# Two buffers instead of one for the activation quantizer of a two-layer transformer kernel

## The chip, the cores and the metric

The kernel runs on the eight cores of one Trainium2 chip, each core on one of the eight sequences of the batch. The metric is the device time of one launch in microseconds (us), taken at the slowest core. The engines of a core are named TensorE (PE in the profile), VectorE (DVE), ScalarE (ACT), GpSimd (POOL) and SyncE (SP), which issues the transfers.

## The reference

A core computes two pre-norm transformer layers on its [2048, 1024] sequence: attention, a feed-forward with one matrix, a latent attention, and a feed-forward with a hidden width of 4096. The part that this case is about is the feed-forward of layer 0, whose input is quantized to whole numbers between -128 and 127 and whose weight is quantized to -1, 0 and 1:

```python
w_scale = jnp.mean(jnp.abs(weight)) + EPS
u = weight / w_scale
w_quant = jnp.clip(jnp.round(u), -1.0, 1.0)
a_scale = jnp.max(jnp.abs(x), axis=-1, keepdims=True) + EPS
z = jnp.clip(x / a_scale * 127.0, -128.0, 127.0)
a_quant = jnp.round(z)
y = jnp.einsum('bsi,oi->bso', a_quant, w_quant)
y = y * (w_scale * a_scale / 127.0)
...
x = x + _L0_attn_ref(_layernorm(x, axis=-1), ...)
x = x + _L0_ffn_ref(_layernorm(x, axis=-1), L0_ffn_weight)
```

## The kernel before

The residual stream stays in SBUF, transposed: eight tiles X0 to X7 of 128 features by 2048 tokens in float32. The kernel emits its stages one after the other, with a barrier of all engines between them: entry (transposes), layer norm and attention of layer 0 (`emit_l0a`), layer norm and feed-forward of layer 0 (`emit_l0f`), and the same two for layer 1. Beside X there is an arena of 104 KB per partition, in which each stage lays its own tiles at offsets written out by hand (`ov`).

Every instruction goes through `do` (line 55), a small recorder. It takes the keys that an instruction reads (`r`) and writes (`w`). For each key it knows the last writers and readers, and puts waits on their semaphores ahead of the instruction. The first writer of a key that the stage has not seen waits for all semaphores of the last barrier (`floor`). Each engine runs its instructions in the order of emission. Keys are names and not addresses, so two tiles can be used independently only if they have two keys. The semaphore counts of an engine are in the order of its instructions.

`emit_l0f` (line 684) first prepares weights, then finds for each token the largest absolute value of the normalized input, and leaves 127 divided by it in a row ROWR. Then comes the loop over four quarters qq of 512 tokens. A quarter begins with a broadcast of its piece of ROWR (TensorE, line 868), which VectorE copies to RAB (line 872). Then come eight steps, c = 0 to 7, one for each tile of 128 features:

- GpSimd makes the scaled input in the tile XN_: subtract the mean (line 313, in the helper `xn_into`), multiply by the inverse deviation (line 317), multiply by RAB (line 878).
- ScalarE adds 128.5 and writes U_ (line 883), and copies U_ to R_ (line 887).
- VectorE takes the whole part off R_ in eight pairs of instructions, for the powers 128, 64, ... 1: line 891 writes to B_ the power where R_ is at least that, line 894 subtracts B_ from R_. What is left in R_ is the fraction, and line 897 writes U_ - 128 - R_, the rounded value, to the slice c of AQW in bfloat16.

After the eight steps TensorE multiplies by the quantized weight WQ: eight output tiles of eight matmuls each (line 907). The first output tile takes each slice of AQW as soon as it is there. VectorE scales each result (line 922, with ASB from line 920) and GpSimd adds it to X (line 925). The next quarter's XN_ stands behind these additions on GpSimd's queue.

XN_, U_, R_ and B_ have one buffer each.

Of the kernel before, what the change touches and what calls it, by code (L numbers as in the profile page):

```python
# [7 lines left out]
F32 = mybir.dt.float32  # L8
BF16 = mybir.dt.bfloat16
AF = mybir.ActivationFunctionType  # L10
OP = mybir.AluOpType
# [4 lines left out]
NCH = 8  # L16
NQ = 4
QW = 512
# [14 lines left out]
class KB:  # L33
# [650 lines left out]
    def emit_l0f(self):  # L684
        s = self
# [6 lines left out]
        SB32 = s.ov("SB32", [32, 128], F32, 57 * 1024)  # L692
        RAB = s.ov("RAB", [128, QW], F32, 58 * 1024)
        ASB = s.ov("ASB", [128, QW], F32, 60 * 1024)
        U_ = s.ov("U_", [128, QW], F32, 62 * 1024)
        ROWR = s.ov("ROWR", [1, 4096], F32, 64 * 1024)
        WPA = s.ov("WPA", [128, T], F32, 82 * 1024)
        R_ = s.ov("R_", [128, QW], F32, 94 * 1024)
# [167 lines left out]
        for qq in range(NQ):  # L866
            s.do("tensor", lambda e, qq=qq, ROWR=ROWR:
                 e.matmul(s.PS[6][:], s.ONE1[0:1, :],
                          ROWR[0:1, QW * qq:QW * (qq + 1)], start=True, stop=True),
                 r=("ROWR", "one1"), w=("PS6",))  # L870
            s.do("vector", lambda e, RAB=RAB:
                 e.tensor_copy(RAB[:], s.PS[6][:]), r=("PS6",), w=("RAB",))
            for c in range(NCH):
                wx = ("XN00", "XN01", "XN02", "XN03") if qq == 0 and c == 0 \
                    else ()
                s.xn_into(XN_[:], "XN", c, qq, eng="gpsimd", wx=wx)
                s.do("gpsimd", lambda e, XN_=XN_, RAB=RAB:
                     e.tensor_tensor(XN_[:], XN_[:], RAB[:], OP.mult),  # L878
                     r=("XN", "RAB"), w=("XN",))
                uwx = ("XN10", "XN11", "XN12", "XN13") if qq == 0 and c == 0 \  # L880
                    else ()
                s.do("scalar", lambda e, U_=U_, XN_=XN_:
                     e.activation(U_[:], XN_[:], AF.Identity,  # L883
                                  bias=s.SM[:, 30:31], scale=1.0),
                     r=("XN", "SM30"), w=("U",) + uwx)
                s.do("scalar", lambda e, R_=R_, U_=U_:
                     e.activation(R_[:], U_[:], AF.Copy), r=("U",), w=("R",))
                for k in range(7, -1, -1):
                    val = float(1 << k)
                    s.do("vector", lambda e, val=val, B_=B_, R_=R_:  # L890
                         e.tensor_scalar(B_[:], R_[:], val, val, OP.is_ge, OP.mult),  # L891
                         r=("R",), w=("B",))
                    s.do("vector", lambda e, R_=R_, B_=B_:
                         e.tensor_tensor(R_[:], R_[:], B_[:], OP.subtract),  # L894
                         r=("R", "B"), w=("R",))
                s.do("vector", lambda e, c=c, U_=U_, R_=R_, AQW=AQW:
                     e.scalar_tensor_tensor(  # L897
                         AQW[:, QW * c:QW * (c + 1)],
                         U_[:], -128.0, R_[:], OP.add, OP.subtract),
                     r=("U", "R"), w=(f"AQc{c}",))  # L900
            for mch in range(NCH):
                bk = f"PS{mch % 2}"
                bank = s.PS[mch % 2]
                for kc in range(NCH):
                    s.do("tensor", lambda e, mch=mch, kc=kc, bank=bank,
                         WQ=WQ, AQW=AQW:
                         e.matmul(bank[:],  # L907
                                  WQ[:, 1024 * kc + 128 * mch:1024 * kc + 128 * (mch + 1)],
                                  AQW[:, QW * kc:QW * (kc + 1)],
                                  start=(kc == 0), stop=(kc == NCH - 1)),  # L910
                         r=("WQ", f"AQc{kc}"), w=(bk,))
                s.close_group(bk)
                if mch == 0:
                    s.do("tensor", lambda e, qq=qq, ROWR=ROWR:
                         e.matmul(s.PS[6][:], s.ONE1[0:1, :],
                                  ROWR[0:1, 2048 + QW * qq:2048 + QW * (qq + 1)],
                                  start=True, stop=True),
                         r=("ROWR", "one1"), w=("PS6",))
                    s.do("vector", lambda e, ASB=ASB:
                         e.tensor_copy(ASB[:], s.PS[6][:]), r=("PS6",), w=("ASB",))  # L920
                s.do("vector", lambda e, bank=bank, ASB=ASB, mch=mch:
                     e.tensor_tensor(s.SC[2 + mch % 2][:], bank[:], ASB[:], OP.mult),
                     r=(bk, "ASB"), w=(f"SC{2 + mch % 2}",))
                s.do("gpsimd", lambda e, mch=mch, qq=qq:
                     e.tensor_tensor(s.X[mch][:, QW * qq:QW * (qq + 1)],
                                     s.X[mch][:, QW * qq:QW * (qq + 1)],
                                     s.SC[2 + mch % 2][:], OP.add),
                     r=(f"SC{2 + mch % 2}", f"X{mch}q{qq}"), w=(f"X{mch}q{qq}",))
# [552 lines left out]
```

How the kernel before makes its waits and increments, by code:

```python
        def f(e, build=build, real=tuple(real), sn_inc=sn_inc, n=n):  # L99
            for (sn, v0) in real:
                e.wait_ge(sems[sn], v0)
            build(e).then_inc(sems[sn_inc], n)
# [19 lines left out]
    def barrier(self):  # L122
        self.flush_ep()
        self.do("sync", lambda e: e.nop(),
                xw=[(sn, self.cnt[sn]) for sn in (*self.LDS, *self.STS)])
        vals = {}
        for e in ENGS:
            vals[e] = self.do(e, lambda en: en.nop(),
                              xw=[(ESEM[e], self.cnt[ESEM[e]])], force=True)
        for e in ENGS:
            for o in ENGS:
                if o == e:
                    continue
                sn = ESEM[o]
                if self.hw[e].get(sn, 0) < vals[o]:
                    self.hw[e][sn] = vals[o]
                    self.th[e].append(
                        lambda en, sn=sn, v0=vals[o]: en.wait_ge(self.sems[sn], v0))
            for sn in (*self.LDS, *self.STS):
                self.hw[e][sn] = max(self.hw[e].get(sn, 0), self.cnt[sn])
        self.floor = {ESEM[o]: vals[o] for o in ENGS}
        for sn in (*self.LDS, *self.STS):
            self.floor[sn] = self.cnt[sn]
```

## Time and profile before

| | us |
|---|---|
| median of 4 timed runs | 8131.44 |
| lowest and highest of them | 7953.81 to 8172.14 |
| the profiled execution | 7675.34 |
| its span on the slowest core (core 5) | 7673.6 |
| the quantizing loop on core 5 | 2508 to 3099 of the span |

The profile is of one execution. Its times are those of the slowest core, counted from the first instruction. "Idle before" is the time an engine stood still ahead of an instruction, and the name behind the arrow is what ended it. The engines' busy shares are averages over stages with different limits.

### The profile page before, as it was taken

Reading aid. Unit: us, or ns where it says so; the run is one execution under the profiler, and the core shown is the slowest. Engines: PE = TensorE matmul, PEld = TensorE weight load, DVE = VectorE, ACT = ScalarE, POOL = GpSimd, SP = SyncE. Lnnn points to the kernel's source line nnn. Section 1 sums busy time; section 2 is a strip of 40 time slices with the busy share of each in tenths; the row PEclk is TensorE's granted clock in tenths of the full one; section 3 lists DMA queues with packets and bytes.
Section 4 is the critical chain, followed back from the end, with each engine's and each line's share of the span. In section 5 each row is a group of like instructions: output and inputs, shape, how many; then the busy total and the mean of one; then the engine's idle time right before and its main releaser. Section 6 shows DMA issues by size and latency. Waiting matters only on the chain.

```text
span 7673.6 us, 101772 instructions; the slowest of 8 cores (7660.7 to 7673.6 us)
## 1 busy us (share of the span) xinstructions
PE 5883.9 (77%) x15346; PEld 2147.0 (28%) x15346; DVE 2296.5 (30%) x3740; ACT 2055.7 (27%) x3076; POOL 616.7 (8%) x580
## 2 busy tenths in 40 slices
PE   6888988889863111769879988898678879789786
PEld 2333333333321000223222322222223323223232
DVE  1333213332105666121111111111133332342323
ACT  1333333333310000103223322232242241332420
POOL 0000000000002222000000000000021120210200
PEclk8888998889975555889889989898889989899896
DMA  1000000000011000000000000000012212122121
GB/s 54 1 1 1 1 1 1 1 1 1 1 42 47 1 0 0 17 1 1 1 7 1 1 1 1 1 1 1 9 61 72 68 61 80 60 67 75 59 75 67
DMA packets 58435, 179.42 MB, mean 23 GB/s; under 512 B 9723, under 2 KB 16294, under 8 KB 57894
## 3 DMA queue, kind: packets, MB, share of 16 engines
q1 hardware_dynamic: 57894, 172.92, 7.2%
q8 instruction: 253, 4.15, 0.2%
q14 instruction: 288, 2.36, 0.1%
HBM read 164.44 MB, written 8.39 MB: 23 GB/s over the span
## 4 chain that ended last, share of the span: by engine, by line
PE 68%; DVE 15%; issue 8%; ACT 4%; DMA 2%; POOL 1%; DVEq 1%; ACTq 0%; SPq 0%; POOLq 0%; PEldq 0%
PE PS L334 16%; PE PS L352 15%; PE PS L1300 11%; PE PS L1236 7%; DVE R__98 L894 3%; PE PS L340 2%; DVE W1L L1202 2%; DVE B__99 L891 2%; PE PS L359 2%; PE PS L279 2%; ACT W1H L1200 1%; PE PS L274 1%; PE PS L1000 1%; PE PS L985 1%; PE PS L945 1%
## 5 line engine op out<-in xcount | busy, mean ns | idle before, releaser
L346 ACT ACTIVATE E<-PS,SM 128x512 f32<-128x512 f32 x1280 | 864.0, 686 | 1361.4 <-PE PS L340 684.0
L363 DVE COPY RBF<-PS 64x512 f32<-64x512 f32 x128 | 88.2, 689 | 2252.4 <-PE PS L359 2183.4
L334 PE MATMUL PS<-QP,KHD 64*128 64x512 f32 x1280 | 746.3, 675 | 10.8 <-issue 10.6
L352 PE MATMUL PS<-E,VFB 128*128 128x512 f32 x1280 | 659.6, 611 | 4.9 <-ACT E L346 4.9
L352 PE MATMUL PS<-E,VFA 128*128 128x512 f32 x1280 | 656.7, 611 | 1.3 <-ACT E L346 1.3
L1236 PE MATMUL PS<-XNH,W1H 128*128 128x512 bf16 x1024 | 437.1, 427 | 184.0 <-ACT W1H L1200 145.1
L1236 PE MATMUL PS<-XNH,W1L 128*128 128x512 bf16 x1024 | 436.5, 426 | 121.2 <-DVE W1L L1202 104.7
L907 PE MATMUL PS<-AQW,WQB 128*128 128x512 bf16 x256 | 79.5, 453 | 500.5 <-DVE AQW L897 500.5
L1268 POOL TENSOR_TENSOR SC<-SC 128x512 f32<-128x512 f32 x128 | 161.6, 1263 | 3485.8 <-PE PS L1236 3437.0
L1236 PE MATMUL PS<-XNL,W1H 128*128 128x512 bf16 x1024 | 431.8, 422 | 0.4 <-DVE XNL L1184 0.2
L1300 PE MATMUL PS<-ACH,W1H 128*128 128x512 bf16 x1024 | 388.9, 380 | 34.6 <-ACT ACH L1279 34.4
L1300 PE MATMUL PS<-ACL,W1H 128*128 128x512 bf16 x1024 | 388.7, 380 | 9.5 <-POOL ACL L1286 4.2
L1300 PE MATMUL PS<-ACH,W1L 128*128 128x512 bf16 x1024 | 388.5, 379 | 0.2
L334 PE MATMUL PS<-QA,KA 128*128 128x512 f32 x640 | 338.0, 623 | 0.0
L334 PEld LDWEIGHTS PS<-QP,KHD 64*128 64x128 f32 x1280 | 204.5, 196 | 471.8 <-issue 469.3
L1220 DVE TENSOR_TENSOR W1L<-W2F,W1H 128x1024 bf16<-128x1024 f32 x128 | 157.3, 1229 | 585.3 <-PE PS L1300 544.1
L334 PE MATMUL PS<-QB,KB 128*128 128x512 f32 x640 | 321.5, 596 | 0.0
L1217 ACT ACTIVATE W1H<-W2F 128x1024 bf16<-128x1024 f32 x128 | 135.1, 1056 | 671.6 <-PE PS L1300 671.6
L352 PEld LDWEIGHTS PS<-E,VFB 128*128 128x128 f32 x1280 | 231.2, 192 | 297.3 <-issue 290.7
L352 PEld LDWEIGHTS PS<-E,VFA 128*128 128x128 f32 x1280 | 232.4, 192 | 290.5 <-issue 284.3
L1202 DVE TENSOR_TENSOR W1L<-W1F,W1H 128x1024 bf16<-128x1024 f32 x127 | 177.2, 1395 | 317.8 <-ACT W1H L1200 255.3
L883 ACT ACTIVATE U__95<-XN__100,SM 128x512 f32<-128x512 f32 x32 | 23.1, 722 | 825.9 <-POOL XN__100 L878 429.9
(235 smaller groups left out, 6783.4 us busy)
## 6 DMA issues: line engine op xcount, KB each, us to landing
W1F<-w1p SPq DMA_DIRECT2D x128, 512.0 KB, 3.5
W2F<-w SPq DMA_DIRECT2D x128, 512.0 KB, 3.9
TM<-x_in SPq DMA_DIRECT2D x16, 512.0 KB, 12.5
WTR<-w0T SPq DMA_DIRECT2D x16, 512.0 KB, 4.1
y_out<-XO SPq DMA_DIRECT2D x16, 512.0 KB, 2.6
WPA<-wo1T SPq DMA_DIRECT2D x16, 256.0 KB, 2.6
WPA<-wuq SPq DMA_DIRECT2D x8, 128.0 KB, 2.0
WPB<-wuk SPq DMA_DIRECT2D x8, 128.0 KB, 2.0
```

What stands on the lines that cost most here:

```text
L279: e.matmul(s.PS[5][:], s.ALL1[:], sq[:], start=(c == 0), stop=(c == NCH - 1)),
L334: e.matmul(s.PS[sb][:], k_lhsT(kc), q_rhs(qq), start=True, stop=not diag),
L340: e.matmul(s.PS[sb][:], s.I128B[:], s.MSK[:, QW * j:QW * (j + 1)], start=False, stop=True),
L346: e.activation(s.E32[eb][:], s.PS[sb][:], AF.Exp, bias=negc),
L352: e.matmul(pvbank[:], v_lhsT(kc), s.E32[eb][:], start=(kc == 0), stop=(kc == kcmax - 1)),
L359: e.matmul(s.PS[6][hs_ctx, :], s.I128[hs_z, hs_z], s.RBF[hs_z, :], start=True, stop=True),
L894: e.tensor_tensor(R_[:], R_[:], B_[:], OP.subtract),
L1202: e.tensor_tensor(w1l[:], w1f[:], w1h[:], OP.subtract),
L1220: e.tensor_tensor(w2l[:, 0:1024], w2f[:], w2h[:, 0:1024], OP.subtract),
L1236: e.matmul(bank[:], lh[:, FCW * kc:FCW * (kc + 1)], rh[:, QW * kc:QW * (kc + 1)], start=(kc == 0 and pi == 0), stop=(kc == 7 and pi == 2)),
L1268: e.tensor_tensor(s.SC[0][:], s.SC[0][:], s.SC[3][:], OP.add),
L1300: e.matmul(s.PS[mch][:], lh[:, 128 * mch:128 * (mch + 1)], rh[:, QW * kc:QW * (kc + 1)], start=(kc == 0 and pi == 0), stop=(kc == 31 and p ...
```

## The change

XN_, U_, R_ and B_ get a second buffer each (XN2, U2, R2, B2), at offsets of the arena that are free in this stage or, for B2 and XN2, held the weight tile WPB that was read out long before. The steps take the buffers in turn, by (8 qq + c) modulo 2, and each buffer has its own key. The first writers of the tiles in WPB's place (step 1 of the first quarter) also wait for WPB's readers. All instructions, their shapes and the order on every engine stay as they are.

```diff
--- before.py
+++ after.py
@@ -692,7 +692,16 @@
         SB32 = s.ov("SB32", [32, 128], F32, 57 * 1024)
         RAB = s.ov("RAB", [128, QW], F32, 58 * 1024)
         ASB = s.ov("ASB", [128, QW], F32, 60 * 1024)
-        U_ = s.ov("U_", [128, QW], F32, 62 * 1024)
+        UP = [s.ov("U_", [128, QW], F32, 62 * 1024),
+              s.ov("U2", [128, QW], F32, 100 * 1024)]
+        RP = [s.ov("R_", [128, QW], F32, 94 * 1024),
+              s.ov("R2", [128, QW], F32, 102 * 1024)]
+        BP = [s.ov("B_", [128, QW], F32, 96 * 1024),
+              s.ov("B2", [128, QW], F32, 24 * 1024)]
+        XNP = [s.ov("XN_", [128, QW], F32, 98 * 1024),
+               s.ov("XN2", [128, QW], F32, 26 * 1024)]
+        U_ = UP[0]
+        XN_ = XNP[0]
         ROWR = s.ov("ROWR", [1, 4096], F32, 64 * 1024)
         WPA = s.ov("WPA", [128, T], F32, 82 * 1024)
         R_ = s.ov("R_", [128, QW], F32, 94 * 1024)
@@ -871,33 +880,40 @@
             s.do("vector", lambda e, RAB=RAB:
                  e.tensor_copy(RAB[:], s.PS[6][:]), r=("PS6",), w=("RAB",))
             for c in range(NCH):
+                p = (qq * NCH + c) % 2
+                Ut, Rt, Bt, XNt = UP[p], RP[p], BP[p], XNP[p]
+                uk, rk, bk_, xk = f"Up{p}", f"Rp{p}", f"Bp{p}", f"XNp{p}"
                 wx = ("XN00", "XN01", "XN02", "XN03") if qq == 0 and c == 0 \
                     else ()
-                s.xn_into(XN_[:], "XN", c, qq, eng="gpsimd", wx=wx)
-                s.do("gpsimd", lambda e, XN_=XN_, RAB=RAB:
-                     e.tensor_tensor(XN_[:], XN_[:], RAB[:], OP.mult),
-                     r=("XN", "RAB"), w=("XN",))
+                if qq == 0 and c == 1:
+                    wx = ("WPB",)
+                s.xn_into(XNt[:], xk, c, qq, eng="gpsimd", wx=wx)
+                s.do("gpsimd", lambda e, XNt=XNt, RAB=RAB:
+                     e.tensor_tensor(XNt[:], XNt[:], RAB[:], OP.mult),
+                     r=(xk, "RAB"), w=(xk,))
                 uwx = ("XN10", "XN11", "XN12", "XN13") if qq == 0 and c == 0 \
                     else ()
-                s.do("scalar", lambda e, U_=U_, XN_=XN_:
-                     e.activation(U_[:], XN_[:], AF.Identity,
+                s.do("scalar", lambda e, Ut=Ut, XNt=XNt:
+                     e.activation(Ut[:], XNt[:], AF.Identity,
                                   bias=s.SM[:, 30:31], scale=1.0),
-                     r=("XN", "SM30"), w=("U",) + uwx)
-                s.do("scalar", lambda e, R_=R_, U_=U_:
-                     e.activation(R_[:], U_[:], AF.Copy), r=("U",), w=("R",))
+                     r=(xk, "SM30"), w=(uk,) + uwx)
+                s.do("scalar", lambda e, Rt=Rt, Ut=Ut:
+                     e.activation(Rt[:], Ut[:], AF.Copy), r=(uk,), w=(rk,))
                 for k in range(7, -1, -1):
                     val = float(1 << k)
-                    s.do("vector", lambda e, val=val, B_=B_, R_=R_:
-                         e.tensor_scalar(B_[:], R_[:], val, val, OP.is_ge, OP.mult),
-                         r=("R",), w=("B",))
-                    s.do("vector", lambda e, R_=R_, B_=B_:
-                         e.tensor_tensor(R_[:], R_[:], B_[:], OP.subtract),
-                         r=("R", "B"), w=("R",))
-                s.do("vector", lambda e, c=c, U_=U_, R_=R_, AQW=AQW:
+                    kwx = ("WPB",) if qq == 0 and c == 1 and k == 7 else ()
+                    s.do("vector", lambda e, val=val, Bt=Bt, Rt=Rt:
+                         e.tensor_scalar(Bt[:], Rt[:], val, val, OP.is_ge,
+                                         OP.mult),
+                         r=(rk,), w=(bk_,) + kwx)
+                    s.do("vector", lambda e, Rt=Rt, Bt=Bt:
+                         e.tensor_tensor(Rt[:], Rt[:], Bt[:], OP.subtract),
+                         r=(rk, bk_), w=(rk,))
+                s.do("vector", lambda e, c=c, Ut=Ut, Rt=Rt, AQW=AQW:
                      e.scalar_tensor_tensor(
                          AQW[:, QW * c:QW * (c + 1)],
-                         U_[:], -128.0, R_[:], OP.add, OP.subtract),
-                     r=("U", "R"), w=(f"AQc{c}",))
+                         Ut[:], -128.0, Rt[:], OP.add, OP.subtract),
+                     r=(uk, rk), w=(f"AQc{c}",))
             for mch in range(NCH):
                 bk = f"PS{mch % 2}"
                 bank = s.PS[mch % 2]
```

The order on ScalarE at the start of the quantizing loop, before: U from XN and R from U, each time the same tiles (the numbers behind the names are those of the allocations).

```order
L883 ACTIVATE U__95<-XN__100,SM 128x512
L887 ACTIVATE R__98<-U__95 128x512
L883 ACTIVATE U__95<-XN__100,SM 128x512
L887 ACTIVATE R__98<-U__95 128x512
L883 ACTIVATE U__95<-XN__100,SM 128x512
```

And with the change, at the same place:

```order
L897 ACTIVATE U__95<-XN__101,SM 128x512
L901 ACTIVATE R__97<-U__95 128x512
L897 ACTIVATE U2_96<-XN2_102,SM 128x512
L901 ACTIVATE R2_98<-U2_96 128x512
L897 ACTIVATE U__95<-XN__101,SM 128x512
```

Nothing moved; every second pair has other tiles. Lines 883, 887, 891, 894 and 897 of before are lines 897, 901, 906, 910 and 913 with the change.

## Rows read from the trace of the kernel before

**Rows 1.** All cores: span and mean granted TensorE clock
```profile
core 2: 7660.7 us, clock 0.853
...
core 5: 7673.6 us, clock 0.850
```

**Rows 2.** Page, part 1: busy time, share of the span, instructions
```profile
PE 5883.9 (77%) x15346; PEld 2147.0 (28%) x15346; DVE 2296.5 (30%) x3740; ACT 2055.7 (27%) x3076; POOL 616.7 (8%) x580
```

**Rows 3.** Groups of instructions, 2500 to 3100 us (busy, mean | idle before <-releaser)
```profile
L907 PE MATMUL PS<-AQW,WQB 128*128 128x512 bf16 x256 | 79.5, 453 | 500.5 <-DVE AQW L897 500.5
...
L891 DVE TENSOR_SCALAR B__99<-R__98 128x512 f32<-128x512 f32 x256 | 142.2, 556 | 102.1 <-ACT R__98 L887 70.2 <-POOL XN__100 L317 6.0 <-ACTq L128 1.8
L897 DVE SCALAR_TENSOR_TENSOR AQW<-U__95,R__98 128x512 bf16<-128x512 f32 x32 | 22.1, 692 | 13.1 <-issue 8.5 <-DVE R__98 L894 4.5
...
L872 DVE COPY RAB<-PS 128x512 f32<-128x512 f32 x4 | 2.8, 691 | 8.3 <-issue 7.0 <-PE PS L868 1.2
```

**Rows 4.** Stretches, core 5: busy time of each engine, clock, DMA
```profile
core 5: us, PE busy (x) PEld busy (x) DVE busy (x) ACT busy (x) POOL busy (x), PEclk, DMA share, GB/s
...
2666.00:2787.00 121.00, 4.97 (x9) 1.20 (x10) 92.03 (x136) 9.69 (x15) 27.14 (x21) 0.50 0.00 0
```

**Rows 5.** Waits, 2500 to 3100 us (waiting <- releaser: total us, times, longest)
```profile
ACT U__95 L883 <- DVE AQW L897: 396.0, 28, 15.1
...
DVE B__99 L891 <- ACT R__98 L887: 70.2, 30, 6.8
```

**Rows 6.** Timeline of a steady step (start, duration, [idle before])
```profile
2679.28 0.69 DVE L897 SCALAR_TENSOR_TENSOR AQW<-U__95,R__98 128x512 bf16<-128x512 f32 x1 [0.17 <-DVE R__98 L894]
2680.11 0.72 ACT L883 ACTIVATE U__95<-XN__100,SM 128x512 f32<-128x512 f32 x1 [13.89 <-DVE AQW L897]
...
2680.98 0.63 ACT L887 ACTIVATE R__98<-U__95 128x512 f32<-128x512 f32 x1
2681.04 1.26 POOL L313 TENSOR_TENSOR XN__100<-X,MU 128x512 f32<-128x512 f32 x1 [10.99 <-ACT U__95 L883]
2681.78 0.80 DVE L891 TENSOR_SCALAR B__99<-R__98 128x512 f32<-128x512 f32 x1 [1.82 <-ACT R__98 L887]
2682.51 1.26 POOL L317 TENSOR_TENSOR XN__100<-XN__100,RBC 128x512 f32<-128x512 f32 x1 [0.20 <-POOL XN__100 L313]
2682.69 1.62 DVE L894 TENSOR_TENSOR R__98<-R__98,B__99 128x512 f32<-128x512 f32 x1
2684.03 1.40 POOL L878 TENSOR_TENSOR XN__100<-XN__100,RAB 128x512 f32<-128x512 f32 x1 [0.26 <-POOL XN__100 L317]
2684.42 1.30 DVE L891 TENSOR_SCALAR B__99<-R__98 128x512 f32<-128x512 f32 x1
2685.82 0.69 DVE L894 TENSOR_TENSOR R__98<-R__98,B__99 128x512 f32<-128x512 f32 x1
...
2694.66 0.69 DVE L897 SCALAR_TENSOR_TENSOR AQW<-U__95,R__98 128x512 bf16<-128x512 f32 x1 [0.17 <-DVE R__98 L894]
```

**Rows 7.** Timeline, VectorE, the step c=7 of the second quarter
```profile
2774.48 0.43 DVE L891 TENSOR_SCALAR B__99<-R__98 128x512 f32<-128x512 f32 x1 [1.82 <-ACT R__98 L887]
2775.01 0.69 DVE L894 TENSOR_TENSOR R__98<-R__98,B__99 128x512 f32<-128x512 f32 x1
...
2785.19 0.69 DVE L897 SCALAR_TENSOR_TENSOR AQW<-U__95,R__98 128x512 bf16<-128x512 f32 x1 [0.17 <-DVE R__98 L894]
```

**Rows 8.** Timeline, start of the second quarter
```profile
2658.76 1.26 POOL L925 TENSOR_TENSOR X<-X,SC 128x512 f32<-128x512 f32 x1 [0.62 <-PE PS L868]
...
2659.98 1.26 POOL L313 TENSOR_TENSOR XN__100<-X,MU 128x512 f32<-128x512 f32 x1
...
2666.40 0.80 DVE L891 TENSOR_SCALAR B__99<-R__98 128x512 f32<-128x512 f32 x1 [6.79 <-ACT R__98 L887]
```

**Rows 9.** Line 363, the copy in the attention
```profile
L363 DVE COPY RBF<-PS x128: 682/689/697, 296.4 to 5423.9; 64x512 f32<-64x512 f32 x128
```

**Rows 10.** Timeline, TensorE, the end of the second quarter
```profile
2788.65 15.23 PE L907 MATMUL PS<-AQW,WQB 128*128 128x512 bf16 x56
```

## The prediction

> **What bounds the kernel now.** I first read the table of cores [rows 1]: all eight spans lie between 7660.7 and 7673.6 us at the same granted clock, about 0.85, so any core stands for all, and I use core 5. The page's busy shares [rows 2] say TensorE 77%, VectorE 30%, ScalarE 27%, GpSimd 8%. Over the whole program TensorE sets the time. But the change touches only the activation quantizer of layer 0's feed-forward, so the limit has to be read there. The groups of that stage [rows 3] show the opposite picture: TensorE's 256 matmuls of line 907 are busy 79.5 us and wait 500.5 us for the quantized tile AQW that VectorE writes on line 897. The table of stretches [rows 4] agrees: from 2666 to 2787 us (the quantizing part of the second quarter) VectorE is busy 92.03 of 121 us, TensorE 4.97, and the granted TensorE clock is 0.50, its level of 1.2 GHz, after an almost idle stretch. So in this stage every microsecond by which VectorE is late is a microsecond of the kernel, as long as it comes to an end in the matmuls at the quarter's end.
>
> What does VectorE wait for? The list of waits [rows 5] gives it in one line: 70.2 us in 30 waits of line 891 for ScalarE's R of line 887. ScalarE in turn waits 396.0 us, 28 times, for VectorE's line 897, since U and R have one buffer each. That is a closed ring: line 897 reads U and R, only then may ScalarE write the next U (0.72 us) and the next R (0.63 us), and only then can line 891 start. The timeline of one steady step [rows 6] shows it: line 897 starts at 2679.28 and ends at 2679.97, U starts at 2680.11, R at 2680.98, and line 891 starts at 2681.78 after an idle time of 1.82 us. The next step's line 897 starts at 2694.66: one step takes 15.38 us.
>
> The same rows show a second cost. The first three VectorE instructions of the step take 0.80, 1.62 and 1.30 us; line 894 later in the step takes 0.69, and where nothing disturbs them the two lines take 0.43 and 0.69 [rows 7]. They are long exactly while GpSimd's three multiplies run (2681.04, 2682.51 and 2684.03), and each ends 0.28 to 0.54 us after the GpSimd instruction that it met. The third GpSimd instruction starts while line 894 still runs and takes 1.40 instead of 1.26. So the two engines take turns, instruction by instruction. The stretch is 0.37 + 0.93 + 0.87 = 2.17 us. The step c=7, in which GpSimd does nothing [rows 7], has no stretch: it runs from 2774.48 to the end of line 897 at 2785.88, that is 11.40 us for the 17 instructions. Check: 1.82 + 11.40 + 2.17 = 15.39.
>
> **The change part by part.** The 17 VectorE, two ScalarE and three GpSimd instructions of a step remain, in the same order and with the same shapes; only the buffers alternate. A quarter has eight steps.
>
> (a) The wait goes. With two U and R, ScalarE can make step c+1's pair while VectorE works on c. Seven times per quarter 1.82 us leave VectorE's path: 12.7 us, and 51.0 us in four quarters. The first step of a quarter keeps its wait [rows 8]: 6.79 us at 2666.40, because its XN stands on GpSimd behind eight residual additions, which wait for the quarter's own matmuls. Nothing there changes. Nor do I see a wait that comes instead: ScalarE's queue holds U, R of c+1 ahead of U of c+2, and only the latter waits for VectorE.
>
> (b) The cover goes for part of GpSimd's work. Before, the first of the three multiplies of a step lay mostly in VectorE's idle time and cost only 0.37 us. Afterwards VectorE is never idle there. GpSimd gets two steps ahead: XN of c+4 is allowed when ScalarE has read XN of c+2, which waits for line 897 of step c. So at the start of a quarter GpSimd makes XN1, XN2, XN3 in one go (nine instructions; the first finds VectorE still waiting for ScalarE), and XN4 to XN7 fall into steps 1 to 4. That leaves 8 + 12 = 20 instructions which meet a busy VectorE, where before 21 met it, seven of them at the small price. The price of one meeting is 0.93 or 0.87 from [rows 6]; I take 0.90. A quarter's stretch is then 20 x 0.90 = 18.0 us against 7 x 2.17 = 15.2 before: 2.8 us more, 11.2 in all. In a formula, a quarter gains 12.7 + 15.2 - 20x. The bounds of x: above, the whole GpSimd instruction, 1.26 [rows 6]; below, the old total, 15.2 / 20 = 0.76. These give gains of 2.7 and 12.7 us a quarter, 11 and 51 in all. I take 0.90 since it is measured on the same pair of instructions.
>
> The Trainium skill ("SBUF — State Buffer", section on the two separate sides) speaks against the change more strongly: it calls the port pair that VectorE and GpSimd share an exclusive lock held for the full instruction, with the loser fully blocked. Taken as worded that is the end at 1.26 and a gain of 11 us instead of some 40; the trace agrees that they exclude each other but shows a price of 0.87 to 0.93, since part of each instruction passes before it is held.
>
> (c) ScalarE now runs U and R (1.35 us a step) beside a working VectorE; before, it ran while VectorE waited. Nothing in this stage shows that meeting. Its bounds: 0, and full exclusion, 28 x 1.35 = 38 us. The nearest row with ScalarE working almost without pause is the copy of line 363 in the attention [rows 9], 682 to 697 ns, mean 689; the copy of the same free size on line 872, with ScalarE idle, takes 691 [rows 3]. That row copies from PSUM, so it is near and not the same. I take 0.
>
> (d) First use of a name. The recorder makes the first writer of a new key wait for all semaphores of the last barrier. In the first quarter line 897 shows 1.07 us of idle time for that in each of eight steps (8.5 us, 8 times) [rows 3]. Those stay. The second B buffer adds one such wait on VectorE at step 1: +1.1 us. The second XN, U and R add theirs on GpSimd and ScalarE, which have over 10 us of slack. Bounds 0 to 4 us for the four keys. The additional waits on WPB's readers are met long before.
>
> (e) TensorE: after step 7 the quarter's last 56 matmuls take 15.23 us [rows 10]; unchanged. The steps before them arrive 11.5 to 14 instead of 15 us apart, still far from keeping TensorE busy.
>
> Sum: -51.0 + 11.2 + 0 + 1.1 = -38.7, say 39 us. The profiled execution took 7675.34 us (span 7673.6 and 1.7 around it), so it would take 7636. The median of the timed runs is 8131.44, 5.9% above that execution, and their own range is 7953.81 to 8172.14. No row shows where those 456 us lie. VectorE's durations do not hang on TensorE's clock, so I subtract the same 39 us: 8092.4, or -0.5%.
>
> **The rivals.** A: GpSimd costs its whole instruction at each meeting (x = 1.26), or ScalarE's 1.35 us are paid in part. Gain 0 to 25 us, time 8106 to 8131. For it: back-to-back instructions leave no gap for either engine. Against it: the two fully overlapped meetings in [rows 6] cost 0.93 and 0.87, with gaps on VectorE of only 0.10.
>
> B, the other side: at step 0 to 4 each GpSimd instruction holds up two VectorE instructions instead of one, because its 1.26 us is longer than line 891 plus its gap (0.53) and VectorE never drains its queue. Place: the 20 meetings of a quarter. Price x = 2 x 0.87 = 1.74, so 27.9 - 34.8 = -6.9 a quarter, 28 us slower, with (d) 29: 8160. It decides from x = 27.9 / 20 = 1.40. Against it: the three stretched instructions of a step are followed by one of 0.69 at once.
>
> C: the wait is removed but comes back, because ScalarE is still held: then line 891 shows 1.8 us again and the time is 8131 to 8132. The ring would have to be closed by another single buffer. AQW has one slice per step, its readers of the quarter before have finished, and SC is not in the ring. I find none.
>
> D: the change is right but the timed runs lie elsewhere. The runs before spread over 218 us, five times the forecast; one of four lies 2.2% under the median. A median of such runs can move by over 2% without any cause in this stage.
>
> **How the numbers follow.** My forecast (25 to 51 us gained): 0.75. A and C together: 0.15. B: 0.04. D: 0.06. The predicted time is 8092.4. About 2% of the time, 163 us, is what a measurement of this kernel can tell from no change; even the complete wait is 51. So faster by over 2% can come only from D (0.04), slower only from D or from B with D (0.02), and 0.94 is left for the middle. The range takes the spread of the runs with it: low 7953.8 - 39 = 7915, high 8172.1 - 6 = 8166, the 6 being a gain at the small end of A.
>
> **What would show it.** Right: line 891 waits for ScalarE four times only, some 20 us in place of 70.2; line 897 starts about 14.2 us apart in steps 1 to 4 and 11.5 in steps 5 to 7; step 0 grows from 13.6 to about 18.6 us with eight stretched instructions; the quarter from the first line 891 to the end of the eighth line 897 shrinks from 119.5 to about 109.6 us. Busy time of lines 891 and 894 grows by about 11 us. Wrong: steps 5 to 7 longer than 11.6 (then ScalarE costs something), stretched instructions over 2.0 us or more than 20 a quarter (rival B), a wait of 1.8 us that remains (rival C), or another stage whose time moved.

## The result and the profile after

| | before, us | changed, us |
|---|---|---|
| first timing, median | 8028.46 (10 runs, the 4 of above among them) | 8094.37 (7 runs) |
| first timing, lowest and highest | 7671.95 to 8172.14 | 7886.93 to 8157.04 |
| first timing, ratio and interval | | 1.0295 [1.0251, 1.0339] |
| later timing (e9), ratio and interval | | 0.9918 [0.9873, 0.9964] |
| lowest time in the three later timings | 7671.33, 7673.51, 7672.18 | 7625.31, 7625.20, 7620.25 |
| profiled execution | 7675.34 | 7903.04 |

The two ratios contradict each other, and the first can't be understood without one fact about the executions: in many executions of either kernel TensorE's granted clock is lower on all four cores of one half of the chip (a die: cores 0 to 3 or 4 to 7), or of both, for a few hundred microseconds or more, and in the first timing every execution of the changed kernel had that, the seven of the table and seven more on record (7834.48 to 8182.49 us), while the profiled execution before had it on no core. The profiled execution of the changed kernel shows it. Its cores, span and mean granted clock:

```profile
core 0: 7893.4 us, clock 0.814
...
core 2: 7668.5 us, clock 0.809
...
core 5: 7743.6 us, clock 0.803
...
core 7: 7901.5 us, clock 0.813
```

All eight cores had 0.850 to 0.853 before [rows 1]. The next two rows are the stretch from the start to just ahead of the changed loop, for core 7 and for core 2 of the same execution (TensorE, its weight loads, VectorE, ScalarE and GpSimd busy, then the granted clock):

```profile
0.00:2500.00 2500.00, 2191.03 (x4346) 846.94 (x4346) 647.93 (x1094) 764.09 (x1177) 87.36 (x76) 0.76 0.02 7
```

```profile
0.00:2490.00 2490.00, 1982.12 (x4533) 787.10 (x4533) 758.45 (x1327) 756.29 (x1177) 141.20 (x195) 0.85 0.04 12
```

Up to here every engine runs the same instructions as before. Core 7 got 0.76 of the clock there and has done less at its end: VectorE has worked through 1094 instructions against 1327 on core 2. Its loop starts 272 us later (first line 906 at 2785.3 against 2513.4), and that is nearly all of the 281 us by which its span exceeds that of a core with the clock of before (7620.8, see e9). So the 7901.5 us of this profile do not come from the instructions of the changed loop. Two stretches of core 7 inside the attention, the first of the kernel before and the second of the changed kernel, show the level of the clock:

```profile
540.00:680.00 140.00, 135.68 (x324) 56.34 (x322) 16.47 (x27) 55.59 (x85) 0.00 (x0) 1.00 0.00 1
```

```profile
590.00:750.00 160.00, 157.44 (x308) 63.32 (x306) 16.41 (x27) 52.50 (x79) 0.00 (x0) 0.81 0.00 1
```

With TensorE busy nearly all the time in both, 1.00 of the clock is granted before and 0.81 here, and 2.3 matmuls a microsecond end before and 1.9 here. Core 2 had the clock of the kernel before up to the loop (0.85 against 0.86 on the same core) and a lower one only behind it (0.82 against 0.89); it is the core on which the loop can be compared.

The groups, on core 2 (lines 906, 910 and 913 are 891, 894 and 897 of before; a group with the second buffers is listed as B, R, U), and TensorE's group on the page (core 7, its loop is 4 us longer):

```profile
L906 DVE TENSOR_SCALAR B__99<-R__97 128x512 f32<-128x512 f32 x128 | 81.4, 636 | 37.4 <-ACT R__97 L901 19.5 <-POOL XN L892 6.0
L906 DVE TENSOR_SCALAR B<-R 128x512 f32<-128x512 f32 x128 | 69.1, 540 | 12.3 <-DVE AQW L913 0.4
...
L913 DVE SCALAR_TENSOR_TENSOR AQW<-U__95,R__97 128x512 bf16<-128x512 f32 x16 | 11.1, 693 | 6.3 <-issue 4.3 <-DVE R__97 L910 2.1
```

```profile
L923 PE MATMUL PS<-AQW,WQB 128*128 128x512 bf16 x256 | 81.7, 469 | 455.5 <-DVE AQW L913 444.6
```

In [rows 3] line 891 was busy 142.2 us and waited 70.2 for R. Now the two groups of line 906 are busy 81.4 + 69.1 = 150.5 us and wait 19.5: the busy time has grown by 8.3, the wait has shrunk by 50.7. The stretches of lines 906 and 910 (what their instructions take beyond 0.43 and 0.69 us) are together 70.4 us, against 58.5 of lines 891 and 894 on core 5 before. TensorE's wait for AQW on VectorE went from 500.5 to 444.6. The waits in the loop, on core 2, answer to [rows 5]:

```profile
ACT U__95 L897 <- DVE AQW L913: 161.0, 12, 14.9
...
ACT U L897 <- DVE AQW L913: 143.3, 12, 13.9
...
DVE B__99 L906 <- ACT R__97 L901: 19.5, 3, 6.5
```

VectorE waits for R three times, at the starts of quarters 2 to 4, for 6.5 us each where it was 6.8 [rows 8]; the other 27 are gone. ScalarE still waits 24 times for VectorE's line 913, as it should: it is now a step ahead. The stretch of the second quarter answers to [rows 4]:

```profile
2653.00:2763.00 110.00, 4.24 (x8) 0.83 (x8) 94.67 (x136) 10.09 (x16) 26.99 (x21) 0.50 0.00 0
```

VectorE is busy 94.67 of 110 us where it was busy 92.03 of 121. A whole step, to be read against [rows 6]:

```profile
2671.73 0.69 DVE L913 SCALAR_TENSOR_TENSOR AQW<-U__95,R__97 128x512 bf16<-128x512 f32 x1 [0.17 <-DVE R__97 L910]
2672.34 0.42 DVE L906 TENSOR_SCALAR B<-R 128x512 f32<-128x512 f32 x1
2672.57 0.72 ACT L897 ACTIVATE U__95<-XN__101,SM 128x512 f32<-128x512 f32 x1 [14.58 <-DVE AQW L913]
...
2672.86 0.69 DVE L910 TENSOR_TENSOR R<-R,B 128x512 f32<-128x512 f32 x1
...
2673.49 1.26 POOL L313 TENSOR_TENSOR XN__101<-X,MU 128x512 f32<-128x512 f32 x1 [7.80 <-ACT U__95 L897]
2673.66 1.38 DVE L906 TENSOR_SCALAR B<-R 128x512 f32<-128x512 f32 x1
2674.96 1.26 POOL L317 TENSOR_TENSOR XN__101<-XN__101,RBC 128x512 f32<-128x512 f32 x1 [0.20 <-POOL XN__101 L313]
2675.14 1.63 DVE L910 TENSOR_TENSOR R<-R,B 128x512 f32<-128x512 f32 x1
2676.49 1.40 POOL L892 TENSOR_TENSOR XN__101<-XN__101,RAB 128x512 f32<-128x512 f32 x1 [0.27 <-POOL XN__101 L317]
2676.88 1.30 DVE L906 TENSOR_SCALAR B<-R 128x512 f32<-128x512 f32 x1
...
2685.79 0.69 DVE L913 SCALAR_TENSOR_TENSOR AQW<-U,R 128x512 bf16<-128x512 f32 x1 [0.17 <-DVE R L910]
```

Line 906 starts at 2672.34, before line 913's recorded end of 2672.42, and U and R are made beside it. GpSimd's three instructions now all meet a working VectorE. The stretched ones are 1.38 (0.95 too long), 1.63 (0.94) and 1.30 (0.87). Each ends 0.28, 0.55 and 0.29 us after the GpSimd instruction that it met, that is its own 0.43 or 0.69 us less some 0.15. From line 913 to line 913 it is 14.06 us instead of 15.38.

The loop, from the first start of line 891 (now 906) to the last start of line 897 (now 913), took 563.1 to 565.3 us on the eight cores before, median 564.1. It takes 517.6 to 519.4 on cores 0 to 5 now, and 522.3 and 522.7 on cores 6 and 7. The gain is 45 to 46 us.

### The profile page after: what moved, and what is told of

The parts are those of the page before. It is cut to its first block, busy times and chain, and to the rows that moved or that the text cites. A ratio compares the mean times of both kernels' runs of the same rounds, so it can differ in the third digit from the quotient of the medians.

```text
span 7901.5 us, 101825 instructions; the slowest of 8 cores (7665.6 to 7901.5 us)
## 1 busy us (share of the span) xinstructions
PE 6180.3 (78%) x15346; PEld 2245.8 (28%) x15346; DVE 2300.6 (29%) x3740; ACT 2062.7 (26%) x3076; POOL 619.9 (8%) x580
## 4 chain that ended last, share of the span: by engine, by line
PE 70%; DVE 14%; issue 8%; ACT 3%; DMA 2%; DVEq 1%; POOL 1%; ACTq 0%; SPq 0%; POOLq 0%; PEldq 0%
PE PS L334 18%; PE PS L352 16%; PE PS L1316 11%; PE PS L1252 7%; PE PS L340 2%; DVE W1L L1218 2%; PE PS L359 2%; PE PS L279 2%; ACT W1H L1216 1%; DVE R__97 L910 1%; PE PS L274 1%; DVE R L910 1%; PE PS L1016 1%; PE PS L1001 1%; PE PS L961 1%
## 5 line engine op out<-in xcount | busy, mean ns | idle before, releaser
L352 PE MATMUL PS<-E,VFB 128*128 128x512 f32 x1280 | 723.2, 664 | 1.5 <-ACT E L346 1.5
L352 PE MATMUL PS<-E,VFA 128*128 128x512 f32 x1280 | 718.7, 663 | 0.8 <-ACT E L346 0.8
L923 PE MATMUL PS<-AQW,WQB 128*128 128x512 bf16 x256 | 81.7, 469 | 455.5 <-DVE AQW L913 444.6
L334 PE MATMUL PS<-QA,KA 128*128 128x512 f32 x640 | 399.9, 726 | 0.0
L334 PE MATMUL PS<-QB,KB 128*128 128x512 f32 x640 | 386.1, 703 | 0.0
L352 PEld LDWEIGHTS PS<-E,VFB 128*128 128x128 f32 x1280 | 253.8, 208 | 328.0 <-issue 320.1
L352 PEld LDWEIGHTS PS<-E,VFA 128*128 128x128 f32 x1280 | 255.1, 208 | 322.4 <-issue 314.3
```

The costliest lines, as they stand in the source:

```text
L334: e.matmul(s.PS[sb][:], k_lhsT(kc), q_rhs(qq), start=True, stop=not diag),
L352: e.matmul(pvbank[:], v_lhsT(kc), s.E32[eb][:], start=(kc == 0), stop=(kc == kcmax - 1)),
```

## The experiments

### Repetitions: e1, e8, e9, e12

e1, e9 and e12 are the changed kernel and e8 the kernel before, unedited, each timed beside the kernel before. e1 ran on another chip than e8 and e9, and e12 on a third.

> The changed kernel once more, unedited, timed in rounds with the kernel before. The comparison so far reads 3% slower, although on the cores with an undisturbed TensorE clock the changed kernel spans 7617 to 7626 us against 7661 to 7674 before, and its quantizing loop takes 518 to 519 us against 563 to 565. Theory 1: the buffers gain 45 us and the 3% is a lower granted clock that falls on some cores in some executions of either kernel, in stages with the same instructions. It expects undisturbed cores again at 7615 to 7630 us (before: 7660 to 7675), a loop of 518 to 520 us on them, and a timed ratio of 0.99 to 1.00 in executions with no disturbed core; how many there will be it can't say. Theory 2: the change itself makes the kernel slower: then undisturbed cores would not repeat at 7620, or the ratio stays at 1.02 to 1.04 with the clock at 0.85 on all cores.

Measured: median 7937.13 us (7625.31 to 8006.59, 8 runs) against 7925.91 (7671.33 to 8106.01, 11 runs). The lowest is 46.0 us below the lowest of before. Loop 517.6 to 519.2 on all eight cores. There is no ratio.

> The kernel before, unedited, timed against itself, to have more executions without a disturbed core and to see how often one is disturbed. Undisturbed executions at 7665 to 7680 us, loop 563 to 565 us. Theory 1 (a lower granted clock falls on some cores of either kernel): a ratio of 1.00, and by the 7 undisturbed of 21 executions so far about one in three undisturbed. Theory 2 (the change makes such executions more frequent, 1 undisturbed of some 22): the same share here, but clearly fewer in the next kernel.

> The changed kernel, unedited, a third time. Undisturbed executions at 7622 to 7632 us against 7665 to 7680, a ratio of 0.993 to 0.995 from those alone. Theory 1 expects about one undisturbed execution in three, theory 2 at most one of eight.

Measured: e8 has a median of 7981.83 us (7673.65 to 8083.51, 7 runs) and a loop of 563.3 to 565.4. e9 has 7876.05 (7625.20 to 8002.73, 13 runs) against 7727.17 (7673.51 to 8062.74, 16 runs), and a ratio of 0.9918 [0.9873, 0.9964]. Three of its 13 runs lie at 7625 to 7627. The cores of e9 with the clock of before:

```profile
core 4: 7614.9 us, clock 0.856
core 5: 7627.3 us, clock 0.853
...
die 1 (median of its cores): 7620.8 us, clock 0.854
```

The median of these four, 7620.8 us, lies 45.4 below the median of the eight spans before (7666.2), which is the gain of the loop.

> The changed kernel, unedited, a fourth time, to narrow the interval of the ratio (0.9918, 0.9873 to 0.9964 in the last timing, 1.0295 in the first). If 45 to 50 of 7675 us are the whole effect, 0.993 to 0.995.

Measured: median 7891.18 us (7620.25 to 8079.7, 8 runs) against 7963.46 (7672.18 to 8123.32, 11 runs), no ratio; the lowest 51.9 below the lowest of before.

What follows: the effect of the change is a gain of 45 to 52 us, 0.6 to 0.7%. In the repetitions the executions without the lower clock on any core are 7671.33 to 7681.95 us before (14 of them, median 7674.7) and 7620.25 to 7626.97 with the change (5 of them, median 7625.3), and the two sets do not touch. A ratio of 1.03 did not come back, and with the clock of before no core of the changed kernel is as slow as before. How often the lower clock falls on the one or the other kernel is not settled. Of the kernel before, 16 of 55 runs lie within 11 us of its lowest; of the changed one, 5 of 36, or 5 of 43 with the seven more of the first timing. That could be chance, or the change could bring the lower clock on more often. e8, the kernel before, had 1 of 7 where the runs beside it had 7 of 16, so such counts scatter, and I claim nothing from them.

### e3: one R

```diff
-                Ut, Rt, Bt, XNt = UP[p], RP[p], BP[p], XNP[p]
-                uk, rk, bk_, xk = f"Up{p}", f"Rp{p}", f"Bp{p}", f"XNp{p}"
+                Ut, Rt, Bt, XNt = UP[p], RP[0], BP[p], XNP[p]
+                uk, rk, bk_, xk = f"Up{p}", "Rp0", f"Bp{p}", f"XNp{p}"
```

> The changed kernel with one R buffer only (XN, U and B keep two). R of the next step can't start before line 897's counterpart has read R, so of the 1.82 us of wait per step only the part for U (0.72 us and its hand-over, about 0.85) is hidden and some 0.95 remains, 28 times: waits of VectorE for R of 26 us plus 20 at the quarters' starts, and a loop of 540 to 548 us. If only the U buffer mattered, it would stay at 519; if R alone mattered, it would go back to 564.

Measured: loop 544.7 to 548.5 us. The waits around VectorE's first instruction and ScalarE's R, on core 7:

```profile
ACT R__97 L901 <- DVE AQW L913: 376.7, 28, 16.4
...
DVE B__99 L906 <- ACT R__97 L901: 30.0, 15, 6.4
...
DVE B L906 <- ACT R__97 L901: 12.5, 14, 0.9
```

28 times R (not U) waits for line 913, and VectorE waits 0.90 us at each step for it: 30.0 + 12.5 = 42.5 us, of which some 19 are the quarters' starts. So the 1.82 us of [rows 6] are U's half and R's half: the second U hides 0.92 us, and the second R, on top of it, the other 0.90. A second R without a second U was not run; by the code R is copied from U, so it would start no earlier.

### e2 and e10: one XN, with one B and with two

```diff
-                Ut, Rt, Bt, XNt = UP[p], RP[p], BP[p], XNP[p]
-                uk, rk, bk_, xk = f"Up{p}", f"Rp{p}", f"Bp{p}", f"XNp{p}"
+                Ut, Rt, Bt, XNt = UP[p], RP[p], BP[0], XNP[0]
+                uk, rk, bk_, xk = f"Up{p}", f"Rp{p}", "Bp0", "XNp0"
```

The diff is that of e2; e10 keeps BP[p] and f"Bp{p}".

> Of the change only U and R keep two buffers; XN and B have one. If the ring of waits runs through U and R alone, the gain stays: a loop of 516 to 521 us, undisturbed cores at 7615 to 7627 us, and up to 2 us less for the first-use wait of the second B that is gone. If GpSimd's lead of a second XN is needed, VectorE waits for ScalarE again at many steps and the loop is over 530 us. The nine GpSimd instructions in a row at a quarter's start should become six at most.

> The changed kernel with one XN buffer; U, R and B keep two. With one XN and one B the loop was 525.8 us against 518.5 with all four doubled. If the 7 us are the lead of the second XN (GpSimd starts the next XN 0.9 us after the last, not at once, and one more of its instructions meets a working VectorE in each quarter), the loop stays at 524 to 527. If they are the single B buffer, it returns to 518 to 520.

Measured: e2 has a loop of 524.7 to 526.3 us and spans of 7626.9 to 7642.9; its one time is 7644.47. My expectation of 516 to 521 missed by some 5. e10 has 523.8 to 526.5, so the 6 to 7 us are mostly the second XN. The second B is not quite nothing: quarters 2 to 4 last 110.1 us each in e2 and 109.4 in e10, since steps of e2 hold pauses of 0.35 us that e10 doesn't have. Where the second XN's part lies can be read at the start of the second quarter of e2:

```profile
2656.76 1.40 POOL L892 TENSOR_TENSOR XN__101<-XN__101,RAB 128x512 f32<-128x512 f32 x1 [0.26 <-POOL XN__101 L317]
...
2658.36 0.72 ACT L897 ACTIVATE U<-XN__101,SM 128x512 f32<-128x512 f32 x1 [4.03 <-POOL XN__101 L892]
...
2659.29 1.27 POOL L313 TENSOR_TENSOR XN__101<-X,MU 128x512 f32<-128x512 f32 x1 [1.13 <-ACT U L897]
```

GpSimd ends XN1 and must wait until ScalarE has read it, so 1.1 us pass before it begins XN2. In the changed kernel that handover costs nothing (XN1 starts at 2652.03, when R0 is not yet made; the next section's rows). Counting VectorE's stretched instructions in steps gives 21 a quarter in e10 instead of 20, and 74.3 instead of 70.4 us of stretch in the loop: 3.9 of the 6 us. The turns between the quarters (end of step 7 to the next line 906) are 26.9 us instead of 26.2 on average, three times, another 2.1. That the ring of waits runs through U and R alone stands; that the whole gain stays without the second XN was wrong.

### e4: what a meeting costs

```diff
-                s.xn_into(XNt[:], xk, c, qq, eng="gpsimd", wx=wx)
-                s.do("gpsimd", lambda e, XNt=XNt, RAB=RAB:
-                     e.tensor_tensor(XNt[:], XNt[:], RAB[:], OP.mult),
-                     r=(xk, "RAB"), w=(xk,))
+                if c < 2:
+                    s.xn_into(XNt[:], xk, c, qq, eng="gpsimd", wx=wx)
+                    s.do("gpsimd", lambda e, XNt=XNt, RAB=RAB:
...
```

> The changed kernel with GpSimd's three instructions left out in steps 2 to 7 of each quarter (these steps quantize the input of step 0 or 1 once more, so the output is another). It prices the meetings of the two engines. Theory of a price near 0.87 to 0.90 us for each of 20 meetings a quarter: 18 of them go (2 in step 0 remain), 4 x 18 x 0.9 = 65 us, a loop of 453 to 458 us. If a meeting costs the whole 1.26 us, the loop falls by 91 to 428; if the long instructions were long for another reason (the first ones after a wait, say), it stays at 519.

Measured: loop 452.8 to 453.4 us, spans 7551.8 to 7560.3. VectorE at the start of the second quarter:

```profile
2636.32 1.09 DVE L907 TENSOR_SCALAR B__99<-R__97 128x512 f32<-128x512 f32 x1 [6.49 <-ACT R__97 L902]
2637.52 1.69 DVE L911 TENSOR_TENSOR R__97<-R__97,B__99 128x512 f32<-128x512 f32 x1
2639.31 0.43 DVE L907 TENSOR_SCALAR B__99<-R__97 128x512 f32<-128x512 f32 x1
2639.84 0.69 DVE L911 TENSOR_TENSOR R__97<-R__97,B__99 128x512 f32<-128x512 f32 x1
```

Two instructions are stretched (1.09 and 1.69), and from the third on everything is 0.43 and 0.69; steps 1 to 7 take 11.38 us each. Against the changed kernel (518.4 in e1, here 453.1, means of the cores) the loop has lost some 65.3 us for 72 instructions of GpSimd, 0.91 us each. So the price of a meeting is that, on average, and not the 1.26 us that GpSimd works. How the two engines take turns can be seen at the start of a quarter of the changed kernel:

```profile
2652.03 1.26 POOL L313 TENSOR_TENSOR XN<-X,MU 128x512 f32<-128x512 f32 x1
...
2653.95 1.10 DVE L906 TENSOR_SCALAR B__99<-R__97 128x512 f32<-128x512 f32 x1 [6.50 <-ACT R__97 L901]
...
2656.25 1.71 POOL L313 TENSOR_TENSOR XN__101<-X,MU 128x512 f32<-128x512 f32 x1
...
2656.94 1.31 DVE L906 TENSOR_SCALAR B__99<-R__97 128x512 f32<-128x512 f32 x1
```

XN1 starts at 2652.03; VectorE's first instruction at 2653.95 takes 1.10. GpSimd's third instruction of XN1 is followed by XN2's first at 2656.25, which takes 1.71 because VectorE holds on until 2656.84. Here GpSimd is the one who waits.

### e5: XN on VectorE

```diff
+            def prep(c, qq=qq):
...
-                s.xn_into(XNt[:], xk, c, qq, eng="gpsimd", wx=wx)
-                s.do("gpsimd", lambda e, XNt=XNt, RAB=RAB:
+                s.xn_into(XNt[:], xk, c, qq, eng="vector", wx=wx)
+                s.do("vector", lambda e, XNt=XNt, RAB=RAB:
...
+            prep(0)
             for c in range(NCH):
+                if c + 1 < NCH:
+                    prep(c + 1)
```

> The changed kernel with the three instructions that make XN on VectorE instead of GpSimd, emitted one step ahead. No meeting is left, so 18.1 us of stretch a quarter go, and 8 x 3 instructions of 0.69 and a gap of 0.10 come, 19.0 us: within a quarter the two are worth the same. At a quarter's start VectorE no longer waits for the three GpSimd instructions behind the last addition, some 3 to 5 us, three times. Loop 505 to 515 us. If a meeting of the engines were dearer than the 0.9 us measured (by delays the rows don't show), the loop falls below 490; if it were free, it rises above 560.

Measured: loop 499.8 to 501.5 us, spans 7598.6 to 7611.0, one time 7612.51. That is below my 505 to 515. The loop is 17.5 us shorter than the changed kernel's, with GpSimd's work done by VectorE. The groups on core 2:

```profile
L918 DVE TENSOR_TENSOR R<-R,B 128x512 f32<-128x512 f32 x128 | 88.6, 692 | 13.3
...
L914 DVE TENSOR_SCALAR B__99<-R__97 128x512 f32<-128x512 f32 x128 | 54.5, 426 | 14.7 <-ACT U L897 1.8 <-DVE R__97 L918 1.4
...
L313 DVE TENSOR_TENSOR XN<-X,MU 128x512 f32<-128x512 f32 x16 | 10.9, 684 | 0.4 <-DVE XN__101 L892 0.4
```

No group is stretched (692 and 426 ns, against 861 and 636 for the first buffers of the changed kernel), and the three instructions of XN are 0.69 each. From its first line 914 to the end of its last line 921, the third quarter takes 104.48 us against 108.67. Only six of the eight XN lie inside it (XN0 and XN1 are made ahead of step 0, where VectorE would wait), so the 19.0 us of my expectation for 24 instructions were too many: 18 instructions with their gaps are 14.2 us, 3.9 less than the 18.1 of the meetings. The turns between the quarters give some 4 us of the 17.5. In this loop the help that GpSimd gives is worth less than nothing to VectorE.

### e7 and e11: no ring and little chain

e7 makes XN on VectorE and puts two instructions in the place of ScalarE's two and VectorE's 17 (the lines of U, R, the eight pairs and AQW go):

```diff
-                s.do("scalar", lambda e, Ut=Ut, XNt=XNt:
...
-                     r=(uk, rk), w=(f"AQc{c}",))
+                s.do("vector", lambda e, Ut=Ut, XNt=XNt:
+                     e.tensor_single_scalar(Ut[:], XNt[:], 12582912.0, OP.add),
+                     r=(xk,), w=(uk,) + uwx)
+                s.do("vector", lambda e, c=c, Ut=Ut, AQW=AQW:
+                     e.tensor_single_scalar(AQW[:, QW * c:QW * (c + 1)],
+                                            Ut[:], 12582912.0, OP.subtract),
+                     r=(uk,), w=(f"AQc{c}",))
```

> A version that removes what the change covers up: the value is rounded by adding and subtracting 12582912 (in float32 that leaves the nearest whole number), two VectorE instructions in place of ScalarE's two and VectorE's 17, and XN is made on VectorE. A step is three instructions of 0.69, one of 0.43 and one of about 0.43 to 0.69, each with a gap of 0.10: 3.4 us instead of 13.6. A quarter is 8 x 3.4 = 27 plus the 20 us of its last matmuls and evictions. If the stage is bound by VectorE as read, the loop (first to last rounding) shrinks from 519 to 165 to 180 us and undisturbed cores span about 7270 us (7250 to 7300). If TensorE's clock or its waits take over, the loop stays above 220.

Measured: loop 176.6 to 178.1 us, spans 7278.9 to 7291.5, median 7464.82 (7289.91 to 7542.83, 5 runs), ratio 0.9475 [0.9398, 0.9552]. One step of VectorE in the second quarter:

```profile
2570.52 0.69 DVE L313 TENSOR_TENSOR XN<-X,MU 128x512 f32<-128x512 f32 x1
2571.38 0.69 DVE L317 TENSOR_TENSOR XN<-XN,RBC 128x512 f32<-128x512 f32 x1 [0.17 <-DVE XN L313]
2572.17 0.69 DVE L892 TENSOR_TENSOR XN<-XN,RAB 128x512 f32<-128x512 f32 x1
2572.97 0.43 DVE L897 TENSOR_SCALAR U<-XN 128x512 f32<-128x512 f32 x1
2573.57 0.43 DVE L900 TENSOR_SCALAR AQW<-U 128x512 bf16<-128x512 f32 x1 [0.17 <-DVE U L897]
2573.91 0.69 DVE L313 TENSOR_TENSOR XN__101<-X,MU 128x512 f32<-128x512 f32 x1
```

A step is 3.39 us. The loop (here from the first line 897 to the last line 900) is 341 us shorter than in the changed kernel, and the spans with an undisturbed clock are about 337 us shorter (7283 against 7621), so what VectorE saves here goes into the kernel's time nearly one to one: the stage is bound by VectorE as read. e7 also has XN on VectorE; against e5, which has that too, the two instructions of rounding alone shorten the loop by 323 us.

e11 is e7 with the two factors of a token multiplied once per quarter. Its edit against e7:

```diff
-                 e.tensor_copy(RAB[:], s.PS[6][:]), r=("PS6",), w=("RAB",))
+                 e.tensor_tensor(RAB[:], s.PS[6][:],
+                                 s.RBC[:, QW * qq:QW * (qq + 1)], OP.mult),
+                 r=("PS6", f"RB{qq}"), w=("RAB",))
...
-                s.xn_into(XNt[:], xk, c, qq, eng="vector", wx=wx)
+                s.do("vector", lambda e, c=c, qq=qq, XNt=XNt:
+                     e.tensor_tensor(XNt[:], s.X[c][:, QW * qq:QW * (qq + 1)],
+                                     s.MU[:, QW * qq:QW * (qq + 1)], OP.subtract),
+                     r=(f"X{c}q{qq}", f"MU{qq}"), w=(xk, *wx))
```

> The version that rounds by adding and subtracting a constant, with the two factors of a token multiplied once per quarter (in the instruction that copied RAB before), so that XN takes two instructions instead of three. A step falls from 3.40 to about 2.6 us: 8 x 0.8 x 4 = 25 us, a loop of 151 to 155 us against 177.8, undisturbed cores at 7255 to 7265 us. If TensorE's matmuls of the first output tile (0.6 us a step, still after each slice) took over as the bound, the gain would stay under 10 us.

Measured: loop 150.0 to 151.5 us, median 7256.47 (7252.76 to 7264.67, 4 runs), ratio 0.9454 [0.9426, 0.9481].

```profile
core 1: 7240.2 us, clock 0.874
...
core 4: 7255.6 us, clock 0.871
```

It is faster than the kernel before by over 5% and, by the lowest times (7252.76 against 7620.25), the changed one by 4.8%. Its loop is 26.6 us shorter than that of e7; the 32 instructions of 0.69 with their gaps are 25.3.

## Why the prediction was right or wrong

**The forecast of the ratio.** I gave 0.94 to "within 2%" and 0.02 to "slower by over 2%". The first timing reads 2.95% slower, outside all that I held likely. The step that failed is the one from the sum to the timed runs. Of the 456 us between the profiled execution and the median I wrote that no row shows where they lie, and then took them to be the same for both kernels and subtracted 39 us. Rival D, the only place where they could differ, got 0.06 in all and mostly pointed towards faster. The runs showed in its place that such a surplus is time with a lower TensorE clock (0.81 granted instead of 1.00), in stages whose instructions the change does not touch: 272 of the 281 us of core 7 in the profiled execution are lost before the loop begins. In e1's timing the kernel before has it as well, at 7848.86 to 8106.01 us. In the first timing it fell on every execution of the changed kernel; three repetitions did not bring the ratio back, and why it fell so that time stays open. The interval of 1.0251 to 1.0339 holds for that one timing and does not cover how the next ones scatter.

The median of 8094.37 next to my 8092.4 is luck: the executions behind it have the lower clock, and the later medians were 7937, 7876 and 7891. The 39 us that I predicted are less than what such a median moves by from timing to timing.

**(a) The wait goes.** Right. 27 of 30 waits went, 50.7 us against the 51.0 of the sum; the three starts stayed (6.5 us, foreseen 6.79). e3 shows that the wait consists of a half for U and a half for R. No wait came back, so rival C is out.

**(b) The meetings.** Right in kind and number: 8 stretched instructions in step 0, 3 in each of steps 1 to 4, none in 5 to 7, in quarters 2 to 4 as forecast. In the first quarter step 0 has 6: there VectorE starts at 2513.37, when GpSimd has already ended XN1 (2512.91). (I called GpSimd's three instructions multiplies; line 313 subtracts.) The price was 0.906 a piece (18.1 us a quarter), forecast 0.90; e4 gives 0.91. In all the stretch grew by 11.9 us, forecast 11.2. Lengths of the steps: 18.47, 14.14 and 11.39 us, forecast 18.6, 14.2 and 11.5. Rival A's 1.26 and rival B's 1.74 are both excluded by e4. The lock that the Trainium skill ("SBUF — State Buffer", section on the two separate sides) describes is seen, and its wording holds. My step from it to a loss of 1.26 us was wrong, and so was my reason for the smaller price. In the step above VectorE's instruction starts 0.17 us after GpSimd's and ends 0.15 us earlier than its own duration after GpSimd's end: 1.26 - 0.17 - 0.15 = 0.94. That 0.15 is the same in all 78 stretched instructions of core 2, so while GpSimd holds it up VectorE gets no further than that.

**(c) ScalarE beside VectorE.** Right: nothing. Step 5 of the second quarter has U and R of a later step beside VectorE and no GpSimd:

```profile
2728.60 0.42 DVE L906 TENSOR_SCALAR B<-R 128x512 f32<-128x512 f32 x1
2728.84 0.72 ACT L897 ACTIVATE U__95<-XN__101,SM 128x512 f32<-128x512 f32 x1 [12.57 <-DVE AQW L913]
...
2729.13 0.69 DVE L910 TENSOR_TENSOR R<-R,B 128x512 f32<-128x512 f32 x1
2729.70 0.63 ACT L901 ACTIVATE R__97<-U__95 128x512 f32<-128x512 f32 x1
```

Lines 906 and 910 take 0.42 and 0.69 beside ScalarE's 0.72 and 0.63.

**(d) First use.** Forecast 1.1 us on VectorE; the first line 906 of step 1 idles 0.45 us in the first quarter, so some 0.5. The trace shows why it is not 1.1: this line 906 waits for nothing that line 913 makes, so its 16 waits begin at 2530.17, while line 913 still runs (to 2530.82).

**The sum.** Forecast a gain of 39, measured 45 to 46 (46.3 between core 5 before and core 2 now, which I take apart here). The four quarters gained 43.8: they last 114.7 and three times 108.65 us, from 125.7, 119.5, 119.5 and 119.8. The term that was mis-sized is (a), which counted the wait of 1.82 and no more. Where VectorE waited 1.82 us it now starts 0.08 before the recorded end of line 913, so such a place gave 1.90, in all 2.2 us more. The first-use wait was 0.6 cheaper, and the larger stretch took 0.7. The remaining 3 us are small ones that I can't all name; pauses of 0.35 in four steps before, absent from those steps on core 2 now, are about half. e2 has such pauses and e10 hasn't, so the second B takes part in that; but e5, with two B, has them in four steps as well, and what makes them stays open. The turns between the quarters, for which I had forecast nothing, gave the other 2.5 us, of which 0.9 are the shorter waits for R (6.50 or 6.52 for 6.8).

## What to carry to other kernels

An engine's share over the whole program says nothing about a stage; a ring of single buffers shows as two waits that name each other with nearly the same count (28 and 30 here), and doubling exactly the tiles in the ring opens it. When the wait goes, ask what it covered: here 12 of the 51 us went into meetings with GpSimd, and work given to GpSimd can cost VectorE more than doing it (e5). And before polishing the handover of a chain of 17 instructions, ask whether the chain is needed: two instructions in its place (e7 against e5) shortened the loop by 323 us, seven times what the buffers gave.

## What the runs showed of the hardware that I had not expected

- Two VectorE instructions of which the second waits for nothing new start 0.08 us before the first one's recorded end (2671.73 + 0.69 and 2672.34); with a semaphore between them the gap is 0.10 to 0.17.
- A GpSimd instruction on two tiles (1.26 us) that meets a chain of VectorE instructions delays it by 0.91 us on average (e4), whether the VectorE instruction has one input tile or two. VectorE's instruction then ends 0.28 us (line 906) or 0.55 us (line 910) after GpSimd's. When GpSimd arrives second it is GpSimd that takes longer, up to 1.72 us.
- Sixteen semaphore waits ahead of an instruction leave the engine idle for 1.07 us even when all but one are met long before (line 913 in the first quarter, 8 times), where three waits leave 0.17 us (the same line later). In the trace the waits stand 0.069 us apart. Where the instruction needs nothing from the one before it, they run beside that one and cost less (0.45 us at line 906).
- The granted TensorE clock can be 0.81 instead of 1.00 for most of a stage with the same instructions (0.76 instead of 0.86 in the mean up to 2500 us, core 7). Beside the levels 1.00 and 0.50 it is a third one, absent on all eight cores of the profiled execution before. The four cores of a die have it together: in every execution on record their mean clocks lie within 0.02 of each other, whatever their spans. The times of this kernel differ by over 6% with it; no experiment here told what brings it about.
